# A decoder layer on one core: maxima issued ahead of operands and rows, the context's transposed text loaded instead of transposed on chip, two copies moved to ScalarE, and the last output split over two banks

## The chip, the core and the metric

The kernel runs on one core of a Trainium2 chip. The core has five engines with a program each: TensorE (PE in the profile, its weight loads PEld), VectorE (DVE), ScalarE (ACT), GpSimd (POOL) and SyncE (SP), which here does nothing but issue transfers on its queue. They meet at semaphores. The metric is the device time of one execution in microseconds (us), as the median of several runs.

## The reference

B = 8 sequences of T = 256 rows with D = 256 columns go through three stages, each followed by a layer norm. All is float32.

```python
x = layernorm(x + attn(x))             # causal attention, 16 heads of 16, with biases
x = layernorm(x + xattn(x, ctx_1024))  # slot attention on a context, 3 iterations
x = layernorm(x + ffn(x))              # 16 experts of 64, the best 4 for each row

# attn: att = softmax(mask(q k^T / 4)); y = att v; y @ w_proj + b_proj
# xattn: Pn = rmsnorm(ctx); k = Pn Wk^T; v = Pn Wv^T
#   3 times: softmax(rmsnorm(slots) Wq^T k^T / 16) over the slots, divided by its
#   sum over the context + 1e-6; updates = attn v; slots = gru(updates, slots)
# ffn: gates = 4 best of sigmoid(x sel^T), normalised; sum of gate * relu(x key_e) value_e
```

## The kernel before

**Precision.** Each float32 operand of a product is kept as two float32r tiles, HI and LO, and a product is three matmuls (`split3`). HI is written by ACT, LO = value - HI by DVE or POOL. A chain of "copy to HI, subtract to LO" stands behind every transposed text.

**Stage 1, attention**, is one long unrolled list of `quad`s: QUADS = 32, four to a sequence, each of three `third`s, with `period, place = divmod(quad, 8)`, so that a period is two sequences. The scores are computed twice. `natural(quad + 4)` makes them with rows on partitions, four quads ahead, and DVE takes the row maxima from them. Once two quads are done, PE transposes the maxima (job "neg", L1906), ACT copies them to `negT` (`maxima_out`, it raises `neg_ok`), and SP moves them as row K_ROWS = 96 of `q_op` (`maxima(hh)`, L519, two transfers of 4 KB for each half sequence hh = quad // 2). `turned(quad)` (L1872, L1876) then makes the scores transposed with the maxima already subtracted by that row. It waits for the maxima's landing at quad = 2 * hh.

`q_op` and `k_op` of sequences 1 to 7 take a way through memory. `write_q(pair, b)` and `write_k(pair, b)` (L489, L490, L497, L498) write three transfers of 256 KB each into `q_rows` and `k_rows`. `operands(n, half)` (L506, L509) waits for both to have landed (`rows_out`) and for the last reader of the buffer (`t_mm`), and then reads 768 KB back. All of this, the input rows (`load_x`, L475) and the maxima are issued by SP in one written order; a wait in it holds up all that stands behind. What SP issues at each quad is set by `place`: at place 0 `operands(2p+1, 1)`, `write_q(p+1, 0)`, `load_x`; at place 1 `write_k(p+1, 0)`; at place 2 `operands(2p+2, 0)`, `write_q(p+1, 1)`; at place 4 `operands(2p+2, 1)`, `load_x`; at place 6 `operands(2p+3, 0)`. After each of the even places stands `maxima(quad // 2 + 1)`.

**Stage 2, slot attention.** For a pair of sequences, `cross(i)` runs UNITS = 6 units u, alternating between the pair's two sequences (j = u % 2). PE computes scores for unit u + 1 (L1991), scales (L2000), the products with the attention weights (`inputs(u)`, L2171), and the state's products (L448). In units 4 and 5 of a pair it also prepares the next pair's context: `context_text(i, j)` transposes the context with four PE transposes (L456) into a PSUM bank, ACT and DVE make `cT_hl` from that bank, and keys and values follow. `c_in` holds the context as loaded; ACT takes squares of it for the norm (`c_sq`). The first pair's context is prepared in the last quads of stage 1 (`first_context`). Banks are handed on by lists (`jobs2`, `FIRST_BANK`): a job waits until the last job's reader in the same bank is done. `scales` (key "rb") and the second `context_text` share bank 1.

**Stage 3, experts.** `experts(i)` runs products with keys, gates and values for a pair. PE transposes x2 by way of a copy `x2f`, written by DVE in `text(i, j)`; for pair 1 this happens in the first `experts` call. The output of a sequence is two products of 24 matmuls, "half" (rows 0 to 127) and "o" (rows 128 to 255), in the two halves of one bank. When both are done, DVE adds x2, takes the moments, POOL makes the inverse deviation, DVE normalises into `y_out` and SP stores.

Of the kernel before, what the change touches and what calls it, by code (L numbers as in the profile page):

```python
# [17 lines left out]
ALU = mybir.AluOpType  # L18
# [4 lines left out]
P = 128  # L23
# [46 lines left out]
def decoder_layer(nc, x, xT, ctx, w_qkv, w_proj, wq, wk, wv, wihT, whhT, eselT, keys, values, cols, lines, out):  # L70
    stack = ExitStack()
    with stack:
# [64 lines left out]
        q_op = sb("q_op", [P, 2, 2, H // 2, T], F32R, where=sq_op)  # L137
# [18 lines left out]
        k_op = sb("k_op", [P, 2, H // 2, T], F32R, where=s1)  # L156
# [112 lines left out]
        rows_ok = sem("rows_ok")  # L269
# [15 lines left out]
        cT_mm, cT_hi, cT_lo = event("cT_mm", 2), event("cT_hi", 2), event("cT_lo", 2)  # L285
# [103 lines left out]
        for u in range(UNITS):  # L389
            jobs2 += (front(u + 1) if 0 < u < UNITS - 1 else front(u + 1)[1:]) + back(u)  # L390
            jobs2 += context(0)[:1] if u == 4 else []
            jobs2 += mid(u + 1) if u + 1 < UNITS else []
            jobs2 += front(UNITS)[:1] + context(0)[1:] + context(1)[:1] if u == 4 else []
        jobs2 += context(1)[1:2] + mid(UNITS)[:1] + context(1)[2:] + [(("uT", 0), 2, x2_ok, 2, 1)] + front(UNITS + 1)[:1]
# [29 lines left out]
        LAST_TEXT = (0, 2)  # L424
        jobs3 = []
# [43 lines left out]
        def _(sp):  # L469
# [43 lines left out]
            def maxima(hh):  # L513
# [3 lines left out]
                after(sp, rows_ok, 2 if hh == 0 else 0)  # L517
# [23 lines left out]
            for quad in QUADS_AND_TAIL:  # L541
# [32 lines left out]
                if quad % 2 == 0 and 0 <= quad // 2 + 1 < 2 * B:  # L574
# [1757 lines left out]
```

## Time and profile before

| what | value |
|---|---|
| median of 3 runs | 668.17 us (667.05 to 669.31) |
| the profiled execution's own time | 666.62 us |
| its span (the profile's times count from its start) | 664.9 us |
| PE busy | 621.7 us, 93% |
| DVE, ACT, POOL busy | 74%, 49%, 34% |
| stage 1 | up to about 233 us |
| stage 2 | about 233 to 545 us |
| stage 3 | from about 545 us |

The rows below come from the page of the profile and from views of its trace. A view of the chain that ended last gives start, duration and what was run or waited for. A timeline gives start, duration, engine, line, operation, output <- input, and in brackets the engine's idle time before it with what ended it. "SPq" is the time in which SP's queue takes in a transfer, not the transfer itself. PEclk is the TensorE clock that was granted, as a share of 2.4 GHz: 1.00 is that level, 0.50 is 1.2 GHz.

### The profile page before, as it was taken

What the parts mean: (1) busy time and instruction counts of PE and PEld (TensorE: products, weight loads), DVE (VectorE), ACT (ScalarE), POOL (GpSimd) and SP (SyncE); (2) the same over time, 40 slices, a digit from 0 to 9 for tenths busy, and PEclk for the clock granted to TensorE, in tenths of its full rate; (3) what the DMA queues carried; (4) which work ended last, traced back from release to release, by engine and by line L of the source; (5) the groups of instructions that cost most, each with busy time, mean ns of one, the idle gap of its engine ahead of it and who ended that gap; (6) DMA issues with size and microseconds to landing.
All of it is one profiled execution on the core that took longest, in us unless ns stands there. A gap on an engine that the chain in (4) does not pass through costs nothing.

```text
span 664.9 us, 13964 instructions
## 1 busy us (share of the span) xinstructions
PE 621.7 (93%) x5064; PEld 565.3 (85%) x5064; DVE 493.7 (74%) x1039; ACT 327.0 (49%) x734; POOL 225.2 (34%) x274
## 2 busy tenths in 40 slices
PE   5988998998999999999999999999999998899996
PEld 4766787776767989999899998999989988799996
DVE  4755474674764788879888799887999888767653
ACT  5444553553575355655556555565566644231320
POOL 9402332432453251422223232232312213352543
PEclk9799898997999999999999999999999999999999
DMA  8634646357400040010000000000000000042240
GB/s 283 203 103 146 173 135 190 93 173 217 121 18 1 1 160 0 2 33 2 0 0 0 32 0 0 0 0 0 0 1 1 1 1 1 16 147 82 80 157 34
DMA packets 31374, 43.34 MB, mean 65 GB/s; under 512 B 3072, under 2 KB 18912, under 8 KB 31328
## 3 DMA queue, kind: packets, MB, share of 16 engines
q1 hardware_dynamic: 31328, 42.73, 21.1%
q8 instruction: 28, 0.46, 0.3%
q14 instruction: 18, 0.15, 0.1%
HBM read 29.39 MB, written 13.21 MB: 64 GB/s over the span
## 4 chain that ended last, share of the span: by engine, by line
PE 56%; DVE 13%; issue 13%; DMA 5%; SPq 5%; POOL 4%; ACT 3%; DVEq 0%; POOLq 0%; ACTq 0%
PE bank L448 26%; PE bank L2171 11%; PE bank L1991 4%; POOL hid_hl L801 3%; DMA k_rows<-k_hl 3%; PE bank L1891 2%; DMA q_op<-negT 2%; PE bank L1977 1%; PE bank L456 1%; PE bank L1849 1%; PE bank L2008 1%; SPq L519 1%; PE bank L1856 1%; PE bank L1872 1%; PE bank L2000 1%
## 5 line engine op out<-in xcount | busy, mean ns | idle before, releaser
L448 PE MATMUL bank<-slots_hl,whhT_hl 128*128 128x256 f32 x864 | 113.1, 284 | 0.0
L448 PEld LDWEIGHTS bank<-slots_hl,whhT_hl 128*128 128x128 f32 x864 | 105.5, 188 | 2.4 <-ACT gate_z L1104 1.0
L1293 DVE TENSOR_REDUCE neg_max<-bank 128x2 f32<-128x512 f32 (+1 forms) x96 | 65.7, 690 | 55.2 <-PE bank L1858 41.3
L2171 PE MATMUL bank<-attn_hl,vg_hl 128*128 128x256 f32 x864 | 105.7, 280 | 0.1
L2171 PEld LDWEIGHTS bank<-attn_hl,vg_hl 128*128 128x128 f32 x864 | 100.9, 188 | 4.3 <-ACT attn_hl L815 3.9
L870 ACT ACTIVATE pT<-bank 128x512 f32<-128x512 f32 x96 | 56.9, 598 | 57.7 <-PE bank L1872 41.7
L682 POOL TENSOR_SCALAR_AFFINE_SELECT pT<-pT 128x512 f32<-128x512 f32 x64 | 40.6, 638 | 117.5 <-ACT pT L870 117.4
L696 POOL TENSOR_TENSOR sq<-sq 128x256 f32<-128x256 f32 x24 | 18.1, 754 | 170.6 <-ACT sq L1089 130.3
L801 POOL TENSOR_TENSOR hid_hl<-hid,hid_hl 128x512 fp32r<-128x512 f32 x32 | 40.9, 1303 | 25.8 <-ACT hid_hl L815 25.7
L448 PE MATMUL bank<-x2T_hl,keys_hl 128*128 128x256 f32 x384 | 48.6, 284 | 0.0
L448 PE MATMUL bank<-values_hl,hid_hl 128*128 128x256 f32 x384 | 47.8, 281 | 0.3 <-DVE x L1567 0.3
L448 PEld LDWEIGHTS bank<-x2T_hl,keys_hl 128*128 128x128 f32 x384 | 46.8, 191 | 0.1
L448 PEld LDWEIGHTS bank<-values_hl,hid_hl 128*128 128x128 f32 x384 | 45.6, 188 | 1.0 <-DVE x L1567 0.5
L1403 DVE RECIPROCAL inv_tot<-tot 128x256 f32<-128x256 f32 x24 | 42.1, 1753 | 0.8
L1872 PE MATMUL bank<-q_op,k_op 128*128 128x512 f32 x64 | 33.3, 526 | 6.7 <-DMA q_op<-negT 6.7
L1991 PE MATMUL bank<-slots_hl,kT_hl 128*128 128x256 f32 x288 | 39.4, 286 | 0.0
L448 PE MATMUL bank<-v_w_hl,cT_hl 128*128 128x256 f32 x288 | 37.2, 285 | 0.0
L448 PEld LDWEIGHTS bank<-v_w_hl,cT_hl 128*128 128x128 f32 x288 | 35.2, 188 | 0.8 <-issue 0.6
L1991 PEld LDWEIGHTS bank<-slots_hl,kT_hl 128*128 128x128 f32 x288 | 35.2, 189 | 0.0
L448 PE MATMUL bank<-xT_hl,wqkv_hl 128*128 128x512 f32 (+1 forms) x120 | 26.8, 371 | 7.8 <-DVE xT_hl L1231 6.9
L1094 ACT ACTIVATE gate_r<-bank,brz_col 128x256 f32<-128x256 f32 x48 | 20.2, 472 | 28.0 <-PE bank L2171 28.0
L815 ACT ACTIVATE hid_hl<-hid 128x512 fp32r<-128x512 f32 x32 | 19.5, 630 | 27.6 <-DVE hid L1765 22.2
(212 smaller groups left out, 1298.2 us busy)
## 6 DMA issues: line engine op xcount, KB each, us to landing
gate_rows<-gate_mem SPq DMA_DIRECT2D x48, 128.0 KB, 3.1
q_rows<-q_hl SPq DMA_DIRECT2D x21, 256.0 KB
k_rows<-k_hl SPq DMA_DIRECT2D x21, 256.0 KB
q_op<-q_rows SPq DMA_DIRECT2D x28, 192.0 KB, 3.2
k_op<-k_rows SPq DMA_DIRECT2D x14, 384.0 KB, 4.4
x_in<-in_x_dram SPq DMA_DIRECT2D x8, 256.0 KB, 6.6
c_in<-in_ctx_dram SPq DMA_DIRECT2D x8, 256.0 KB, 4.8
out_dram<-y_out SPq DMA_DIRECT2D x8, 256.0 KB, 2.8
```

What stands on the lines that cost most here:

```text
L448: mm = pe.matmul(dst, left(a), right(b), start=first and n == 0, stop=last and n == 2, skip_group_check=True)
L682: pool.affine_select(out=tile, in_=tile, compare_op=ALU.is_ge, fill=0.0, base=0, pattern=[[0, 4], [1, P]], channel_multiplier=-1).then_inc ...
L696: pool.tensor_tensor(sq[:, 0, :], sq[:, 0, :], sq[:, 1, :], ALU.add).then_inc(sq_sum, 1)
L801: pool.tensor_tensor(hid_hl[:, j, LO, 2 * g:2 * g + 2, :], hid[:, n % HIDDEN, :, :], f32(hid_hl[:, j, HI, 2 * g:2 * g + 2, :]), ALU.subtra ...
L815: return act.activation(dst, src, ACT.Copy, **kw)
L870: act.activation(dst, bank[2 + (3 * quad + third) % 2][:, :].rearrange("p (h n) -> p h n", h=4 if third == 2 else 2), ACT.Exp).then_inc(ex ...
L1094: r = act.activation(gate_r[:, c, :], halves(4)[:, c, :], ACT.Tanh, scale=0.5, bias=brz_col[:, c:c + 1])
L1293: dve.tensor_reduce(dst, src, AX.X, ALU.max, negate=True).then_inc(max_ok, 1)
L1403: dve.reciprocal(inv_tot[:, :], tot[:, :]).then_inc(it_ok, 1)
L1872: mm = pe.matmul(halves(b), k_op[:, n % 2, pair_of(quad, third), 0:P], q_op[:, n % 2, :, pair_of(quad, third), :], start=True, stop=True)
L1991: mm = pe.matmul(halves(b)[:, t, :], kT_hl[:, j, k_part, c, t * P:(t + 1) * P], slots_hl[:, j, s_part, c, :], start=n + t + c == 0, stop=n ...
L2171: mm = pe.matmul(halves(b)[:, m, :], vg_hl[:, j, v_part, 3 * t + r, q:q + P], attn_hl[:, j, at_part, t, :], start=n == 2 and a + m + t == ...
```

## The change

Four things change.

1. In SP's list, at places 0 and 4, `maxima` stands ahead of `operands`, `write_q` and `load_x`; at places 2 and 6 it stays behind them. `q_op` and `k_op` have 97 partitions in place of 128, so that two memsets of POOL and a wait of SP and PE for them (`rows_ok`) fall away.
2. `context_text` is gone from PE (8 blocks of four transposes). The host gives the transposed context too (`ctxT`), and SP loads it over the context in `c_in` once the squares are taken (`turned_context`, 8 more transfers of 256 KB). ACT and DVE make `cT_hl` from `c_in`, and the banks that the transposes used are no longer in the lists.
3. The two `x2f` copies for pair 1 move from DVE in the first `experts` to ACT in unit 4 of the last `cross`.
4. For the last sequence, the product "o" goes to bank 4 (`LAST_BANK`) in place of the second half of bank 3, and DVE adds x2 and takes the moments of each half by itself (`last_output`).

```diff
-        q_op = sb("q_op", [P, 2, 2, H // 2, T], F32R, where=sq_op)
+        q_op = sb("q_op", [K_ROWS + 1, 2, 2, H // 2, T], F32R, where=sq_op)
...
+            def turned_context(i, j):
+
+                sp.wait_ge(c_sq, due(2, i, j + 1))
+                sp.sem_inc(passed, 1)
+                sp.dma_start(c_in[:, j, :, :], rows(ctxT[i * 2 + j, :, :], NC)).then_inc(cT_arr[j], 16)
...
+                if quad in (QUADS - 6, QUADS - 5):
+                    turned_context(0, quad - (QUADS - 6))
+                if place in (0, 4) and 0 <= quad // 2 + 1 < 2 * B:
+                    maxima(quad // 2 + 1)
                 if place == 0:
                     if 1 <= 2 * period + 1 < B:
                         operands(2 * period + 1, 1)
...
-                if quad % 2 == 0 and 0 <= quad // 2 + 1 < 2 * B:
+                if place in (2, 6) and 0 <= quad // 2 + 1 < 2 * B:
                     maxima(quad // 2 + 1)
...
             def context_text_hi(r, j, first=False):
-                act.wait_ge(cT_mm, due(2, r, 2 + j + 1))
+                act.wait_ge(cT_arr[j], due(1, r, 2, step=16))
                 act.wait_ge(vg_mm, due(6, r, 6 + 3 * j))
-                copy(cT_hl[:, HI, :, :], halves(context_bank(("cT", j), first))).then_inc(cT_hi, 1)
+                copy(cT_hl[:, HI, :, :], c_in[:, j, :, :]).then_inc(cT_hi, 1)
...
                         expert_text_hi(0, 1, FIRST_TEXT[1])
+
+                        act.wait_ge(ss_mm, due(UNITS, i, UNITS))
+                        act.wait_ge(sc_ok, due(UNITS, i, UNITS))
+                        act.wait_ge(x2_ok, due(2, 1, 2))
+                        for j in range(2):
+                            copy(x2f[:, j, :, :], x2[:, (2 + j) * NT:(3 + j) * NT, :]).then_inc(xf_ok, 1)
...
+            def last_output(i):
+
+                def linked():
+                    dve.wait_ge(expert_chain, i * EXPERT_LINKS + next_link())
+                dve.wait_ge(y_ok, due(2, i, 1))
+                for t, (signal, count, b) in enumerate(((last_half, 1, 3), (o_mm, due(2, i, 2), LAST_BANK))):
+                    dve.wait_ge(signal, count)
+                    dve.tensor_tensor(u3[:, t, :], halves(b)[:, t, :], x2[:, i * (2 * NT) + NT + t, :], ALU.add).then_inc(expert_chain, 1)
+                    linked()
+                    dve.bn_stats(stats3[:, t, :], u3[:, t, :]).then_inc(expert_chain, 1)
+                    linked()
+                    dve.bn_aggr(mv3[:, t, :], stats3[:, t, :]).then_inc(expert_chain, 1)
+                    linked()
...
-                if first:
-                    text(1, 0)
-                    text(1, 1)
...
-                    if u == 4 and not last:
-                        context_text(i, 0)
...
-                        context_text(i, 1)
```

SP's list at quads 6, 8 and 9 (places 6, 0 and 1), before; `q_op<-negT` are the maxima:

```order
45 L519 DMA q_op<-negT 1x4x256 x2
46 L506 DMA q_op<-q_rows 48x2x512 x2
47 L509 DMA k_op<-k_rows 96x2x512
48 L489 DMA q_rows<-q_hl 8x16x512 x2
49 L490 DMA q_rows<-q_hl 8x16x512
50 L475 DMA x_in<-in_x_dram 128x2x256
51 L519 DMA q_op<-negT 1x4x256 x2
52 L497 DMA k_rows<-k_hl 8x16x512 x2
53 L498 DMA k_rows<-k_hl 8x16x512
```

The same place of SP's list after the change:

```order
44 L519 DMA q_op<-negT 1x4x256 x4
45 L507 DMA q_op<-q_rows 48x2x512 x2
46 L510 DMA k_op<-k_rows 96x2x512
47 L490 DMA q_rows<-q_hl 8x16x512 x2
48 L491 DMA q_rows<-q_hl 8x16x512
49 L476 DMA x_in<-in_x_dram 128x2x256
50 L498 DMA k_rows<-k_hl 8x16x512 x2
51 L499 DMA k_rows<-k_hl 8x16x512
```

The two transfers of `maxima(5)` have moved from behind seven transfers of 256 KB or so to in front of them (x4 is `maxima(4)` and `maxima(5)` side by side); their wait for `neg_ok` moves with them. The same happens at the other quads of place 0 and at those of place 4.

PE's list in units 4 and 5 of a `cross` in the loop, before:

```order
517 L1977 MATMUL bank<-mean_col,sq 128x1 x2
518 L448 MATMUL bank<-cT_hl,qk_w_hl 128x256 x12
519 L448 MATMUL bank<-v_w_hl,cT_hl 128x256 x36
520 L456 MATMUL bank<-ident,c_in 128x128 x4
521 L1991 MATMUL bank<-slots_hl,kT_hl 128x256 x12
522 L1943 REGISTER_ALU
523 L2000 MATMUL bank<-ident,s_rs 128x128 x2
524 L2171 MATMUL bank<-attn_hl,vg_hl 128x256 x36
```

And after:

```order
512 L2001 MATMUL bank<-mean_col,sq 128x1 x2
513 L1976 REGISTER_ALU
514 L449 MATMUL bank<-cT_hl,qk_w_hl 128x256 x12
515 L449 MATMUL bank<-v_w_hl,cT_hl 128x256 x36
516 L2015 MATMUL bank<-slots_hl,kT_hl 128x256 x12
517 L2024 MATMUL bank<-ident,s_rs 128x128 x2
518 L2192 MATMUL bank<-attn_hl,vg_hl 128x256 x36
```

The four transposes between the context's values and the scores are gone, as are the four behind `inputs(4)`; the order of the rest is as it was.

DVE's list at the end of the program, before (from the last sequence's addition to its norm):

```order
640 L1805 TENSOR_TENSOR u<-bank,x 128x512
641 L1549 BN_STATS stats<-u 128x6 x2
642 L1554 BN_AGGR mv<-stats 128x2 x2
643 L1557 TENSOR_SCALAR std<-mv 128x2
644 L1567 TENSOR_SCALAR y_out<-u,mv,std 128x256 x2
```

And after:

```order
638 L1769 TENSOR_TENSOR u<-bank,x 128x256
639 L1771 BN_STATS stats<-u 128x6
640 L1773 BN_AGGR mv<-stats 128x2
641 L1769 TENSOR_TENSOR u<-bank,x 128x256
642 L1771 BN_STATS stats<-u 128x6
643 L1773 BN_AGGR mv<-stats 128x2
644 L1775 TENSOR_SCALAR std<-mv 128x2
645 L1580 TENSOR_SCALAR y_out<-u,mv,std 128x256 x2
```

The first three rows now wait for "half" alone, so that only the second three and what follows stand behind the last product.

## Rows read from the trace of the kernel before

**Rows 1.** The page, busy time, share and instructions of each engine.
```profile
PE 621.7 (93%) x5064; PEld 565.3 (85%) x5064; DVE 493.7 (74%) x1039; ACT 327.0 (49%) x734; POOL 225.2 (34%) x274
```

**Rows 2.** The chain that ended last, 86 to 113 us: start, duration, what.
```profile
87.52 0.32 SPq L506
...
95.46 0.62 SPq L497
...
96.79 5.73 DMA k_rows<-k_hl
...
107.53 3.89 DMA q_op<-negT
```

**Rows 3.** Who waited for whom: us in total, times, longest.
```profile
PE bank L1872 <- DMA q_op<-negT: 6.7, 3, 2.5
```

**Rows 4.** Timeline of PE at the waits of stage 1.
```profile
111.46 0.50 PE L1872 MATMUL bank<-q_op,k_op 128*128 128x512 f32 x1 [2.46 <-DMA q_op<-negT]
...
184.31 0.66 PE L1849 MATMUL bank<-k_op,q_op 96*128 96x128 f32 x4
```

**Rows 5.** Timeline of ACT, the copies that raise `neg_ok` at place 0.
```profile
41.11 0.36 ACT L815 ACTIVATE negT<-bank 8x256 fp32r<-8x256 f32 x1
...
89.80 0.36 ACT L815 ACTIVATE negT<-bank 8x256 fp32r<-8x256 f32 x1
...
135.68 0.36 ACT L815 ACTIVATE negT<-bank 8x256 fp32r<-8x256 f32 x1
...
178.62 0.36 ACT L815 ACTIVATE negT<-bank 8x256 fp32r<-8x256 f32 x1
```

**Rows 6.** Issues of the maxima by SP: ns, least, median, most.
```profile
L519 SPq DMA_DIRECT2D q_op<-negT x32: 573/606/1752, 32.7 to 194.9; - x32
```

**Rows 7.** The chain that ended last, 48 to 60 us.
```profile
51.21 6.55 DMA k_rows<-k_hl
```

**Rows 8.** Timeline of SP, operands of periods 2 and 3.
```profile
133.40 0.79 SPq L506 DMA_DIRECT2D q_op<-q_rows  x2
...
177.17 0.43 SPq L509 DMA_DIRECT2D k_op<-k_rows  x1
```

**Rows 9.** The page, transfers: count, KB each, us from issue to landing.
```profile
k_op<-k_rows SPq DMA_DIRECT2D x14, 384.0 KB, 4.4
```

**Rows 10.** Stretches: length, PE busy (count), PEclk, DMA share, GB/s.
```profile
96.00:98.00 2.00, 2.00 (x28) 1.00 0.51 150
...
162.00:163.00 1.00, 1.00 (x6) 0.50 0.91 266
```

**Rows 11.** Timeline of DVE and PE in units 4 and 5 of the first `cross`.
```profile
295.11 1.53 DVE L1362 SCALAR_TENSOR_TENSOR vg_hl<-bank,c_rs,vg_hl 128x512 fp32r<-128x512 f32 x3
295.94 0.60 PE L456 MATMUL bank<-ident,c_in 128*128 128x128 f32 x4
...
296.30 1.62 PE L1991 MATMUL bank<-slots_hl,kT_hl 128*128 128x256 f32 x12
...
298.26 0.43 PE L2000 MATMUL bank<-ident,s_rs 128*128 128x128 f32 x2 [0.35 <-DVE cT_hl L1231]
```

**Rows 12.** Timeline at the first context, end of stage 1.
```profile
196.01 0.60 ACT L815 ACTIVATE cT_hl<-bank 128x512 fp32r<-128x512 f32 x1 [0.76 <-PE bank L456]
...
197.14 1.09 PE L1921 MATMUL bank<-ident,a_sb 128*128 128x128 f32 x8 [0.71 <-ACT a_sb L815]
```

**Rows 13.** Timeline around the `x2f` copies and their new place.
```profile
542.43 0.84 ACT L1094 ACTIVATE gate_r<-bank,brz_col 128x256 f32<-128x256 f32 x2 [0.49 <-PE bank L2171]
...
562.47 0.85 DVE L1747 COPY x2f<-x 128x512 f32<-128x512 f32 x2
...
568.69 3.10 PE L448 MATMUL bank<-values_hl,hid_hl 128*128 128x256 f32 x24 [0.32 <-DVE x L1567]
```

**Rows 14.** Timeline of DVE behind the last product.
```profile
658.58 0.69 DVE L1805 TENSOR_TENSOR u<-bank,x 128x512 f32<-128x512 f32 x1 [1.82 <-PE bank L448]
659.30 0.75 DVE L1549 BATCH_NORM_STATS2 stats<-u 128x6 f32<-128x256 f32 x2
```

More of the change, by code:

```diff
@@ L155, in decoder_layer @@
         x_in = sb("x_in", [P, 2, NT, D], where=s1)
-        k_op = sb("k_op", [P, 2, H // 2, T], F32R, where=s1)
+        k_op = sb("k_op", [K_ROWS + 1, 2, H // 2, T], F32R, where=s1)
         v_aug = sb("v_aug", [P, 3, NT, H, 2 * DH], where=s1)
@@ L268, in decoder_layer @@
         spot_in, spot_ok = sem("spot_in"), sem("spot_ok")
-        rows_ok = sem("rows_ok")
+        last_half = sem("last_half")
         set_mm, set_q, set_k = sem("set_mm"), sem("set_q"), sem("set_k")
@@ L284, in decoder_layer @@
         c_sq, c_mean, c_rstd, c_kept = event("c_sq", 2), event("c_mean", 2), event("c_rstd", 2), event("c_kept", 1)
-        cT_mm, cT_hi, cT_lo = event("cT_mm", 2), event("cT_hi", 2), event("cT_lo", 2)
+        cT_arr = [event(f"cT_arr{j}", 1, 16) for j in range(2)]
+        cT_hi, cT_lo = event("cT_hi", 2), event("cT_lo", 2)
         kT_mm, kT_hi, kT_lo = event("kT_mm", 2), event("kT_hi", 2), event("kT_lo", 2)
@@ L653, in _ @@
             for batch in range(2):
-                pool.memset(f32(k_op[K_ROWS:, batch, :, :]), 1.0).then_inc(consts, 1)
+                pool.memset(f32(k_op[K_ROWS:K_ROWS + 1, batch, :, :]), 1.0).then_inc(consts, 1)
             pool.wait_ge(consts, 16)
@@ L658, in _ @@
             pool.wait_ge(consts, 19)
-            for e in range(2):
-                pool.memset(f32(q_op[K_ROWS:, 0, e, :, :]), 0.0).then_inc(rows_ok, 1)
-            pool.wait_ge(rows_ok, 2)
             def rstd(i, var, ev, std, k, slot):
@@ L1148, in cross @@
                         expert_text_hi(0, 1, FIRST_TEXT[1])
+                        act.wait_ge(ss_mm, due(UNITS, i, UNITS))
+                        act.wait_ge(sc_ok, due(UNITS, i, UNITS))
+                        act.wait_ge(x2_ok, due(2, 1, 2))
+                        for j in range(2):
+                            copy(x2f[:, j, :, :], x2[:, (2 + j) * NT:(3 + j) * NT, :]).then_inc(xf_ok, 1)
                 if not last:
@@ L1346, in context_text_lo @@
                 dve.wait_ge(cT_hi, due(2, r, 2 + j + 1))
-                sub_hi(cT_hl[:, LO, :, :], halves(context_bank(("cT", j), first)), cT_hl[:, HI, :, :]).then_inc(cT_lo, 1)
+                sub_hi(cT_hl[:, LO, :, :], c_in[:, j, :, :], cT_hl[:, HI, :, :]).then_inc(cT_lo, 1)
             def context_keys_lo(r, j, first=False):
@@ L1747, in text @@
                 dve.tensor_copy(x2f[:, j, :, :], x2[:, bass.ds(i * (2 * NT) + j * NT, NT), :]).then_inc(xf_ok, 1)
+            def last_output(i):
[10 more added lines that the diff above has]
+                    linked()
+                dve.tensor_scalar(std3[:, 0, :], mv3[:, :, 1], LN_EPS, None, ALU.add).then_inc(var3, 1)
+                dve.wait_ge(stored[1], due(1, i, 1, back=1, step=16))
+                normal(i, lambda t: u3[:, t, :], mv3, std3, rstd3, 2, lambda t: y_out[:, 1, t, :], y_ok)
             def experts(i, last, first=False):
@@ L1802, in experts @@
                         route(i, i + 1, 1)
+                    if j and last:
+                        last_output(i)
+                        return
                     dve.wait_ge(o_mm, due(2, i, j + 1))
@@ L1868, in turned @@
                     pe.wait_ge(neg_in[hh % 2], 32 * (hh // 2 + 1))
-                    after(pe, rows_ok, 2 if hh == 0 else 0)
                 after(pe, exp_ok, fill - 1)
@@ L1944, in free_bank @@
                 return b
-            def context_text(r, j, first=False):
-                b = free_bank(r, ("cT", j), first)
-                pe.wait_ge(c_arr[j], due(1, r, 2, step=16))
-                transpose4(pe, b, lambda t, c: c_in[:, j, t, c * P:(c + 1) * P]).then_inc(cT_mm, 1)
             def context_keys(r, j, first=False):
@@ L2024, in first_context @@
             def first_context(quad):
[L2026 to L2028 removed]
+                if quad == QUADS - 3:
                     context_keys(-1, 0, True)
@@ L2275, in experts @@
                         pe.wait_ge(h_lo, due(8, i, 4 * j + 4))
+                        if last and j == 1 and t == 1:
+                            b = LAST_BANK
                         for m in range(NH):
@@ L2280, in experts @@
                             mm.then_inc(o_mm, 1)
+                        elif last and j == 1:
+                            mm.then_inc(last_half, 1)
             experts(0, False, True)
```

33 lines of the change are left out of this document (14 added, 19 removed).

## The prediction

> **What bounds the kernel now.** I read the page first. PE is busy 93% of the span [rows 1], so most of stages 2 and 3 is PE's own work, and what is left to win or lose there is a few tenths at each place where PE idles. Then I read who waits for whom. In stage 1 PE has one kind of wait on a transfer: L1872, `turned`, waits for the maxima three times, 6.7 us in total [rows 3]. The timeline shows the second of them, 2.46 us, ended at 111.46 [rows 4]; the three stand at quads 4, 12 and 20. The chain that ended last shows what such a wait hangs on. From 87.52 to 107.53 it runs through SP and the transfers and not through PE at all [rows 2]: SP issues operands of sequence 3, then rows of q, then x, then rows of k at 95.46; the rows of k land at 96.79 + 5.73 = 102.52; only then may SP issue the operands of sequence 4, behind them more rows of q and, last, `maxima(6)`, whose landing at 107.53 + 3.89 = 111.42 lets PE go on. So in stage 1 each period has one serial chain on SP's queue, and it starts with the `operands` of place 0.
>
> **The change part by part.**
>
> *Maxima ahead at place 0.* The maxima that the change brings forward (hh = 5, 9, 13 and 1) are not those that PE waits for: these (hh = 2, 6, 10) are issued at place 2, where the order stays. So the gain of having the others earlier is 0. The price is their wait. At quad 8 SP issued `operands` at 87.52 [rows 2], but `neg_ok` comes only with the copy at 89.80 + 0.36 = 90.16 [rows 5]. SP must now sit there, then issue two maxima of 0.606 us each [rows 6], and reaches `operands` at about 91.4: 3.9 us later. Period 2 is the same: 133.40 [rows 8] becomes 135.68 + 0.36 + 1.21 = 137.25 [rows 5, 6], 3.9 us later. Behind the `operands` stand `write_q`, `load_x` and `write_k`, and for them waits all that follows to `maxima(6)` and PE.
>
> How much of 3.9 us reaches PE? The lower bound is SP's own time. Before, the seven transfers took SP from 87.52 to 93.03 (the issue of the maxima) and `write_k` went at 95.46. After, the same 5.5 us from 91.4 end at 96.9, 1.4 us after 95.46. The upper bound is 3.9 us, if the queue's data and not the issue sets the landing. For this speaks that 768 KB of operands, 768 KB of q, 256 KB of x and 768 KB of k, 2.56 MB, went from 87.52 to 102.52, which is 171 GB/s, while in 96 to 98, where only writes of rows are left, the queue does 150 GB/s with a DMA share of 0.51 [rows 10]. It was working all the way. I take 3.9 for each of the two periods: **+7.8** (bounds 2.8 and 7.8).
>
> Which of the two bounds holds is where the Trainium skill has a say. Its page "DMA: Bandwidth & Descriptors", section "Two DMAs through the same engine are not ordered", says that in one queue of a DMA engine descriptors start in order; the section "Why a DMA increments its semaphore by 16 and not by 1" says that a transfer whose slowest dimension is 8 uses 8 of the 16 engines. The share of 0.51 agrees with the second. By both, rows of k can't pass rows of q on the same eight engines, and the cost is the upper bound; by the issue times alone it would be the lower one.
>
> *Period 0.* `maxima(1)` went at 41.11 + 0.36 = 41.47 at the earliest [rows 5], and now `operands(1, 1)` and `write_q(1, 0)` stand behind it, from 42.7. By the rate above, the 2.3 MB of operands, q and k take 13.5 us, up to 56.2. The rows of k landed at 51.21 + 6.55 = 57.76 anyway [rows 7], since k itself was late. So 0, and 0.5 as upper bound.
>
> *Quad 24.* `operands(7, 1)` moves by 178.62 + 0.36 + 1.21 = 180.2 against a start 0.83 ahead of 177.17 [rows 5, 8], 3.9 us. Its `k_op` then is issued at 181.1 and lands 4.4 us later [rows 9], at 185.5, while PE's `natural(30)` wanted it at 184.31 [rows 4]. **+1.2** (0.6 to 2.2). At place 4 the operands also move by 2 to 4 us, but they have two quads, over 8 us, until their reader: 0. The memsets and `rows_ok` are 0: the first maxima were issued at 32.7 [rows 6], far behind POOL's start-up. 97 partitions in place of 128 change no count of columns: 0.
>
> *Transposes off PE, in the loop (3 pairs).* Behind the transposes the scores start 296.30 - 295.94 = 0.36 us later [rows 11]. Behind the scores the scales waited 0.35 us for DVE's `cT_hl` because the two shared bank 1 [rows 11]; this wait is gone. The 0.36 us of unit 4's block comes too, but not at this place: the scores need bank 3, whose reader, the first of three DVE instructions from 295.11, ends after 0.75 at 295.9, and that time doesn't come from PE. So the scores start at 295.9 in place of 296.30 and `inputs(5)` 0.4 + 0.35 = 0.75 us earlier, three times: **-2.2** (-1.2 to -3.2, the latter if unit 4's block counts in full). The loads that replace them are issued behind `c_sq`, some 8 us ahead of their use, against landings of about 5 us: hidden. If they were not, each would stand before `cT_hl` for its lateness.
>
> *First context.* ACT waited 0.76 us for PE's transposes, and PE then 0.71 us for the `a_sb` that ACT makes behind them [rows 12]. **-0.6** (0 to -0.7). The second block, at 212.9, is hidden behind ACT's queue: 0. The 512 KB more at quads 26 and 27 run beside an empty queue.
>
> *x2f to ACT.* DVE loses 0.85 us at 562.47 [rows 13]. PE waits for a DVE norm at 568.69, so nearly all of it counts. ACT gains 1.2 us of copies just ahead of `gate_r` at 542.43, where it had 0.49 us to spare: 0.7 us late. DVE behind it has short idles, and PE works on other products meanwhile: 0 to 0.3. **-0.6** (-0.8 to +0.3).
>
> *Last output.* Behind the last product one addition of 128x256 in place of 128x512 and one of two statistics are left: half of 0.69 and half of 0.75 [rows 14]. **-0.7** (-0.3 to -0.8).
>
> **The sum.** 7.8 + 1.2 - 2.2 - 0.6 - 0.6 - 0.7 = +4.9 us against the profiled execution's own 666.62, so 671.5. The median of the runs stands 1.55 above that execution; with the same +4.9 it gives **673.1 us**. I forecast slower by 0.7%.
>
> **The rivals.**
>
> *Rows land by their own issue (ends faster).* The mechanism is in `write_k` of periods 1 and 2. Its landing came 102.52 - 95.46 = 7.06 us after its first issue, with all of q and x just ahead, and 51.21 + 6.55 with an empty queue was no quicker. If that is its own latency, and if SP's slow issues there (5.5 us for seven) were due to a full queue and shrink to 0.6 us each, `write_k` is issued at 91.4 + 4.2 = 95.6, as before. The 7.8 then is 0, quad 24 keeps its 1.2, and the time is 668.17 + 1.2 - 4.1 = 665.3. It decides from the point where 1.8 MB pass in under 5.6 us, which is 320 GB/s against the 150 seen with rows.
>
> *Half of it.* The issue bound: 2.8 + 1.2 - 4.1 = -0.1, 668.1, no change that one can measure.
>
> *The clock.* PE's longer waits of over 6 us (2.46 + 3.9) in place of 2.5. After the third wait of before the granted clock stood at 0.50, the 1.2 GHz level, still at 162 to 163, five us behind the end of the wait [rows 10]. Five us at half rate give 2.5 us more work time. If the second wait, and the new one at quad 26, get such a stretch in full, add about 2.5 to 3: 676. The page "TensorE: Matmul & The Clock Gate" of the Trainium skill, section "HAM oscillation", says that PE's idle gaps cost the clock anew each time; by it this rival is the likelier the longer the waits. Against it: the clock falls already in the shorter waits of before, so most of the price is in the old time.
>
> **How the numbers follow.** 0.60 for the sum as worked out (673.1, itself 670.5 to 675.5), 0.15 for the clock on top (676), 0.15 for rows by their own issue (665.3), 0.10 for half of it (668.1). The range must hold 0.8: it reaches from 666.5, which leaves out most of the faster case, to 677.5. A measurement of this kernel can't tell changes under some 0.3%, 2.0 us. Faster by more: 0.15. Within: 0.12, the half case and the low edge of the sum. Slower: 0.73.
>
> **What would show it.** In the changed trace: SP's issue of `operands` at quads 8 and 16 right behind the maxima and 3.9 us later against `t_mm`; rows of k landing over 9 us after their issue; PE's waits at L1872 of some 6 us for hh = 6 and 10 and an unchanged one for hh = 2; a new wait of about 1 us at `natural(30)`; in the loop no idle before the scales; the last norm some 0.7 us nearer to the last product. The forecast is wrong if the rows land 7 us after their issue as before, or if SP reaches `write_k` without delay; it is too low if PE's clock stays at its lower level for longer behind the waits.

## The result and the profile after

| what | before | changed |
|---|---|---|
| median | 667.44 us (6 runs, 665.71 to 669.31) | 672.30 us (6 runs, 671.36 to 675.35) |
| ratio | 1 | 1.0081, 95% interval 1.0053 to 1.0109 |
| span of the profiled execution | 664.9 us | 669.8 us |

The changed kernel is slower by 0.8%, 4.9 us both in the medians and in the spans. The forecast was 0.7%, +4.9 us. The agreement to a tenth of a us is luck, since the interval alone is nearly 2 us to either side. In this trace quad 24, period 0 and stage 3 each came out 1.8 to 2.7 us away from their terms, and these errors cancelled; the experiments below are mostly about those. An execution at a lower clock throughout (one of the kernel before, and the profiled one of run 10) does not enter the ratios.

The page of the changed kernel, busy time of each engine, against [rows 1]:

```profile
PE 620.0 (93%) x5016; PEld 563.3 (84%) x5032; DVE 493.9 (74%) x1038; ACT 328.0 (49%) x736; POOL 223.2 (33%) x272
```

PE's busy time falls by 1.7 us and its idle time grows by 6.6 us (43.2 to 49.8), so the loss is waiting. The busy time falls by less than the transposes took (32 matmuls, eight blocks like the 0.60 us of [rows 11]), because PE also ran longer at the lower level of the clock: the mean granted clock is 0.977 against 0.982, which is some 7 us more at 0.50, an estimate from these two means and spans. Who waited for whom in the changed kernel (us in total, times, longest), against the one row of [rows 3]:

```profile
PE bank L1901 <- DMA q_op<-negT: 7.2, 3, 3.2
PE bank L1879 <- DMA k_op<-k_rows: 7.2, 3, 3.0
```

L1901 is the old L1872, `turned`, and waits hardly longer than before (7.2 us for 6.7). New is L1879, `natural`, which waits for `k_op` three times. The timeline of PE has all six (start, duration, in brackets the wait):

```profile
66.19 0.49 PE L1901 MATMUL bank<-q_op,k_op 97*128 97x512 f32 x1 [0.97 <-DMA q_op<-negT]
...
108.63 0.66 PE L1879 MATMUL bank<-k_op,q_op 96*128 96x128 f32 x4 [3.00 <-DMA k_op<-k_rows]
...
112.56 0.80 PE L1901 MATMUL bank<-q_op,k_op 97*128 97x512 f32 x1 [3.03 <-DMA q_op<-negT]
...
158.27 1.11 PE L1879 MATMUL bank<-k_op,q_op 96*128 96x128 f32 x4 [2.54 <-DMA k_op<-k_rows]
...
162.57 0.80 PE L1901 MATMUL bank<-q_op,k_op 97*128 97x512 f32 x1 [3.19 <-DMA q_op<-negT]
...
191.17 0.66 PE L1879 MATMUL bank<-k_op,q_op 96*128 96x128 f32 x4 [1.63 <-DMA k_op<-k_rows]
```

The chain that ended last shows why, in the stretch that answers to [rows 2]:

```profile
87.20 0.36 ACT negT L822
...
87.58 0.57 SPq L519
...
88.20 0.57 SPq L519
...
88.89 0.37 SPq L507
...
94.69 1.13 SPq L498
...
96.49 6.97 DMA k_rows<-k_hl
...
108.64 3.88 DMA q_op<-negT
```

SP now waits for ACT's copy, issues the two maxima, and starts the operands at 88.89. At this place the changed kernel is 2.57 us ahead of the one before (quad 10's `turned` at 102.32 in place of 104.89), so 88.89 is 91.46 in the old count: 3.9 us later than 87.52, as forecast. The rows of k land at 96.49 + 6.97 = 103.46, that is 106.03 against 102.52, 3.5 us later.

How far the changed kernel is behind, from the starts of the same instruction in both timelines of PE, gives the whole account (clock 0.50 is the 1.2 GHz level):

| place | before | changed | behind | what happened there |
|---|---|---|---|---|
| `turned` of quad 4, its wait over | 67.31 | 66.19 | -1.12 | wait 0.97 for 1.78 |
| next `turned` | 71.10 | 68.45 | -2.65 | no stretch at clock 0.50 |
| `turned` of quad 12 | 111.46 | 112.56 | +1.10 | 3.00 + 3.03 for 2.46 |
| next `turned` | 115.03 | 116.66 | +1.63 | longer at clock 0.50 |
| `turned` of quad 20 | 157.38 | 162.57 | +5.19 | 2.54 + 3.19 for 2.50 |
| `turned` before `natural(30)` | 181.64 | 186.80 | +5.16 | |
| first `turned` of quad 28 | 192.90 | 201.39 | +8.49 | wait 1.63, then clock 0.50 |
| first `tot` product of stage 2 | 228.01 | 235.86 | +7.85 | first context, -0.64 |
| the same, last pair | 487.12 | 492.09 | +4.97 | loop, -2.88 |
| products with `eselT` | 567.28 | 571.06 | +3.78 | `x2f`, -1.2 |
| last values | 647.50 | 653.05 | +5.55 | clock 0.50 once, gates |
| end | 664.9 | 669.8 | +4.9 | last output, -0.65 |

### The profile page after: what moved, and what is told of

The parts are those of the page before. It is cut to its first block, busy times and chain, and to the rows that moved or that the text cites. A ratio compares the mean times of both kernels' runs of the same rounds, so it can differ in the third digit from the quotient of the medians.

```text
span 669.8 us, 13895 instructions
## 1 busy us (share of the span) xinstructions
PE 620.0 (93%) x5016; PEld 563.3 (84%) x5032; DVE 493.9 (74%) x1038; ACT 328.0 (49%) x736; POOL 223.2 (33%) x272
## 4 chain that ended last, share of the span: by engine, by line
PE 50%; DVE 15%; issue 14%; DMA 6%; SPq 5%; ACT 5%; POOL 4%; DVEq 0%; another core or an unknown queue 0%; ACTq 0%; POOLq 0%
PE bank L449 22%; PE bank L2192 9%; PE bank L2015 4%; DMA k_rows<-k_hl 3%; POOL hid_hl L808 3%; DMA q_op<-negT 2%; PE bank L1920 2%; PE bank L1901 1%; PE bank L2001 1%; PE bank L2032 1%; PE bank L1879 1%; PE bank L457 1%; DVE gate_r L1656 1%; SPq L519 1%; PE bank L1886 1%
## 5 line engine op out<-in xcount | busy, mean ns | idle before, releaser
L1901 PE MATMUL bank<-q_op,k_op 97*128 97x512 f32 x64 | 34.1, 539 | 7.2 <-DMA q_op<-negT 7.2
```

Of the source, the lines that this page charges most:

```text
L1901: mm = pe.matmul(halves(b), k_op[:, n % 2, pair_of(quad, third), 0:P], q_op[:, n % 2, :, pair_of(quad, third), :], start=True, stop=True)
```

## Experiments

Every ratio is to the kernel before, from runs on the same chip, with its 95% interval. All but the fourth keep the three other edits of the change and alter only SP's list; the edit of each is given against the changed kernel, that of the fourth against the kernel before. Single executions of the kernel before lie between 661.8 and 671.9 us, so a trace is one draw; its intervals and waits are worth more than its span. In each expectation, "theory" is what the author held likelier and "rival" the other reading.

### 1. The old order of the maxima, the other edits kept

```diff
-                if place in (0, 4) and 0 <= quad // 2 + 1 < 2 * B:
+                if quad % 2 == 0 and (quad in ()) and 0 <= quad // 2 + 1 < 2 * B:
...
-                if place in (2, 6) and 0 <= quad // 2 + 1 < 2 * B:
+                if quad % 2 == 0 and not (quad in ()) and 0 <= quad // 2 + 1 < 2 * B:
```

> The changed kernel with SP's maxima behind operands and rows at every place, as before; the other three edits stay. My theory: all of the loss is in this order. The changed trace stands 7.85 us behind at the first scale of stage 2; without it this goes and the first context's 0.6 stays, the loop gives 2.9 back, the tail 0.6, stage 3 loses about 0.5 at a DVE gate: 667.4 - 3.6 = 663.8, faster. Rival, the loss comes from the 768 KB or so of added context traffic and the edits on ACT: 668 or more. In the trace: SP's operands at quad 8 within 0.1 us of PE's release again, waits of PE for maxima three times 1.8 to 2.5, none for k_op.

Measured: 661.70 us, ratio 0.9932 (0.9901 to 0.9962). The theory's 663.8 (0.995) is inside the interval, the rival's 668 is not. The order costs 1.0081 / 0.9932 = 1.5%, 10 us, and the other edits together give 4.6 us; they were not run one by one. In the trace PE waits only at `turned` again, three times, 2.01, 3.10 and 3.12 us, the last two longer than the 2.5 us expected.

### 2. Maxima ahead at quad 0 alone

The edit is that of the first run with `(quad == 0)` in place of `(quad in ())`.

> As the first run, but the maxima of quad 0 alone stay ahead. The changed trace came 2.65 us earlier at the second half sequence of pair 1 (quad 4's wait 0.97 in place of 1.78, and no stretch of PE at the lower clock behind it). If the early maxima of quad 0, and the later operands and rows of q behind them, make that gain, this run is 2.3 to 2.7 us under the first: about 661.3, the fastest so far. Rival, that the shorter wait is scatter of one execution: equal to the first run within 0.5 us, 663.8.

Measured: 660.77 us, 0.9922 (0.9894 to 0.9950). 0.9 us under the first run, less than the intervals can tell. The traces settle more. The wait at quad 4 was 1.26 here and 0.97 in the changed kernel, but 2.00 in run 4, which has the maxima of quad 0 ahead too. With the old order at quad 0 it was 1.78 before, 2.01 in run 1, 1.68 in run 3, 2.25 in run 5, 0.56 in run 7, 1.35 in run 9 and 1.36 in run 11: the scatter of this wait is as large as the effect. What it costs depends on a step. The products behind it in the kernel before and in run 3 (timelines of PE, `wqkv` products behind the wait):

```profile
67.87 2.91 PE L448 MATMUL bank<-wqkv_hl,xT_hl 128*128 128x256 f32 x12
```

```profile
67.14 1.68 PE L449 MATMUL bank<-wqkv_hl,xT_hl 128*128 128x256 f32 x12
```

The same twelve matmuls took 2.91 us behind the wait of 1.78 and 1.68 behind the wait of 1.68. In the traces with waits of 1.78, 2.01 and 2.25 there they ran at the lower level of the clock, in the one with 2.00 (run 4) in part, 2.41 us, and in all those with up to 1.68 at the upper. So the -2.65 of the account is 0.3 of start, 0.8 of wait and 1.5 of clock, and it is luck of one execution as much as a gain of the change.

### 3. Maxima ahead at quads 8 and 16 alone

The edit is that of the first run with `(quad in (8, 16))`.

> As the first run, but maxima ahead at quads 8 and 16 alone. Theory, the queue's data sets when rows of k land: each period loses 3.6 us between quad 4 and quad 12's end, 7.2 in all, so 671.0. Rival, SP's own issue sets it: 1.4 each, 2.8 in all, 666.6. In the trace: PE waits at natural for k_op and at turned for maxima at quads 12 and 20, together some 5.5 us in each period.

Measured: 668.11 us, 1.0031 (1.0004 to 1.0058): 6.4 us over the first run, 3.2 for each period. The theory's 7.2 lies 0.8 off, the rival's 2.8 lies 3.6 off, outside the interval. PE's waits in this run:

```profile
109.81 0.83 PE L1879 MATMUL bank<-k_op,q_op 96*128 96x128 f32 x4 [3.13 <-DMA k_op<-k_rows]
...
113.73 0.79 PE L1901 MATMUL bank<-q_op,k_op 97*128 97x512 f32 x1 [2.64 <-DMA q_op<-negT]
...
159.76 0.66 PE L1879 MATMUL bank<-k_op,q_op 96*128 96x128 f32 x4 [3.43 <-DMA k_op<-k_rows]
...
163.80 0.80 PE L1901 MATMUL bank<-q_op,k_op 97*128 97x512 f32 x1 [3.14 <-DMA q_op<-negT]
```

### 4. The kernel before, with the new order alone

```diff
+                if place in (0, 4) and 0 <= quad // 2 + 1 < 2 * B:
+                    maxima(quad // 2 + 1)
                 if place == 0:
...
-                if quad % 2 == 0 and 0 <= quad // 2 + 1 < 2 * B:
+                if place in (2, 6) and 0 <= quad // 2 + 1 < 2 * B:
```

> The kernel before with the new order of maxima alone. Theory: stage 1 loses what it lost in the changed kernel, 7.85 plus the 0.5 that the first context gave back, and nothing returns later: 667.4 + 8.3 = 675.7. Rival, half of the loss needs the new context traffic at quads 26 and 27: 673 or less.

Measured: 679.95 us, 1.0195 (1.0148 to 1.0242), 9.9 to 16 us of loss. The rival falls: the loss needs none of the other edits. But the median is 4 us over the forecast, outside the interval, so the theory's size is not met either. Its trace waits for `k_op` at the same three quads:

```profile
112.96 0.66 PE L1851 MATMUL bank<-k_op,q_op 96*128 96x128 f32 x4 [2.32 <-DMA k_op<-k_rows]
...
163.12 1.11 PE L1851 MATMUL bank<-k_op,q_op 96*128 96x128 f32 x4 [2.92 <-DMA k_op<-k_rows]
...
196.00 0.66 PE L1851 MATMUL bank<-k_op,q_op 96*128 96x128 f32 x4 [1.78 <-DMA k_op<-k_rows]
```

All of its 13.2 us stand at the first `tot` product of stage 2 (241.22 for 228.01), and nothing is added later. Of these, 2.2 stand already at the first `turned` of quad 0 (42.15 for 39.91). This start lies between 39.33 and 42.15 in the traces, without regard to the order (42.13 in run 9, whose list is the old one up to there), so this part is scatter of one execution. Why 11 remain, where the changed kernel lost 7.85 + 0.64, is not shown.

### 5. The wait without the issues

On top of the edit of the first run:

```diff
+                if quad in (8, 16):
+                    sp.wait_ge(neg_ok, quad // 2 + 2)
                 if place == 0:
```

> As the run with the old order, but at quads 8 and 16 SP waits for neg_ok ahead of operands and issues nothing there; the maxima stay behind. It tells the price of the wait from that of the two issues. Theory, the queue's data sets the landing and every us of late start counts: start 2.64 later instead of 3.85, and the run with maxima ahead at the same quads lost 6.4 by 7.7 of late start, so 2 x (2.64 - 0.65) = 4.0: 0.9932 + 0.0060 = 0.999 of before, 665.7. Rival, SP's issue time sets it, and the wait is taken up by issues that were slow on a full queue: 0.5 or less, 662.2.

Measured: 667.21 us, 1.0011 (0.9985 to 1.0038), 5.3 us over the first run by the ratios. The theory's 0.999 is inside the interval, the rival's 662.2 (0.994) is not. Compared with the 6.4 of run 3 the wait by itself is most of the price, but the two do not lose it at the same places: here `maxima(5)` and `maxima(9)` went out late behind seven transfers, and PE waited for them at quads 10 and 18 (the first and the third row), while its wait at quad 12 (the second) shrank to 1.21:

```profile
101.03 0.50 PE L1903 MATMUL bank<-q_op,k_op 97*128 97x512 f32 x1 [1.29 <-DMA q_op<-negT]
...
114.12 0.49 PE L1903 MATMUL bank<-q_op,k_op 97*128 97x512 f32 x1 [1.21 <-DMA q_op<-negT]
...
147.99 0.49 PE L1903 MATMUL bank<-q_op,k_op 97*128 97x512 f32 x1 [2.21 <-DMA q_op<-negT]
```

So putting the maxima first does buy something once SP waits anyway. In the old order their readers had time to spare.

### 6. Maxima ahead where PE waits for them, place 2

The edit is that of the first run with `(quad == 0 or place == 2)`.

> Maxima ahead of operands at quad 0 and at place 2 (quads 2, 10, 18, 26, those for which PE waits at quads 4, 12 and 20), behind them elsewhere. SP idles at place 2 until rows of k land (96.8 to 102.5), while neg_ok comes at 100.1, so the maxima cost the operands nothing and land before PE's turned. Theory: PE's three waits of 2.0, 3.1 and 3.1 go, and part of the half clock behind them: 660.8 - 8 = 652 to 654, ratio 0.98. Rival, natural takes the wait over: k_op lands just when PE wants it (issue 104.3, wanted 108.8), so its landing is later by the 1.2 of issues: gain 4 or less, 657 and up.

Measured: 662.58 us, 0.9940 (0.9913 to 0.9968). The theory falls; even the rival's 4 us did not come. The three waits for maxima at quads 4, 12 and 20 are gone, and these stand in their place:

```profile
75.44 0.66 PE L1879 MATMUL bank<-k_op,q_op 96*128 96x128 f32 x4 [0.48 <-DMA k_op<-k_rows]
...
107.23 0.66 PE L1879 MATMUL bank<-k_op,q_op 96*128 96x128 f32 x4 [0.73 <-DMA k_op<-k_rows]
...
119.99 1.12 PE L1879 MATMUL bank<-k_op,q_op 96*128 96x128 f32 x4 [3.68 <-DMA k_op<-k_rows]
...
167.82 1.11 PE L1879 MATMUL bank<-k_op,q_op 96*128 96x128 f32 x4 [4.09 <-DMA k_op<-k_rows]
```

SP's timeline of this run shows what the wait at 119.99 hangs on (start, duration, issue):

```profile
98.41 1.29 SPq L519 DMA_DIRECT2D q_op<-negT  x2
101.92 0.79 SPq L507 DMA_DIRECT2D q_op<-q_rows  x2
...
108.83 1.16 SPq L499 DMA_DIRECT2D k_rows<-k_hl  x1
110.30 1.91 SPq L507 DMA_DIRECT2D q_op<-q_rows  x2
112.26 0.43 SPq L510 DMA_DIRECT2D k_op<-k_rows  x1
```

The maxima cost nothing, as said: they went out at 98.41 while SP had to wait until 101.92 for rows. But behind them stand the second sequence's rows of q and k (`write_q` of place 2 and `write_k` of place 3, which the list of places above leaves out), issued up to 109.99. The operands of place 4 follow them at once, from 110.30, and their `k_op`, issued at 112.26, landed 7.7 us later, at 119.96; at place 0 and place 2 this took 4.1 and 4.4. In run 1 the `k_op` of place 4 was as slow, 7.2 us (114.73 to 121.9), but there PE had been held up at quad 12 and wanted it only at 122.59. Here it was at `natural(18)`, in quad 14, from 116.31 on. The wait at `turned` was hiding this one.

### 7 and 8. load_x behind write_k

On top of the edit of the first run (run 7) and of the sixth (run 8):

```diff
                     if 1 <= period + 1 < PAIRS:
                         write_q(period + 1, 0)
-                    if 2 <= 2 * period < B:
-                        load_x(2 * period)
-                elif place == 1 and 1 <= period + 1 < PAIRS:
-                    write_k(period + 1, 0)
+                elif place == 1:
+                    if 1 <= period + 1 < PAIRS:
+                        write_k(period + 1, 0)
+                    if 2 <= 2 * period < B:
+                        load_x(2 * period)
```

> As the run with the old order, but load_x of place 0 is issued behind write_k of place 1, so 256 KB are out of the way of rows of k. Theory, the queue's data: 256 KB at 176 GB/s are 1.5 us, rows of k land that much earlier, PE's waits at quads 12 and 20 are 1.6 in place of 3.1: 661.7 - 2.9 = 658.8. Rival, rows land 7 us after their own issue: write_k waits for nothing but SP and is issued 0 to 1.4 us earlier; if it is not (k_lo sets it), nothing: 661.7.

> Both: maxima ahead at quad 0 and place 2, load_x behind write_k. Theory: once PE waits for no maxima, k_op just in time is next, and 1.5 us more slack there give 0 to 1 us: 652 to 653. Rival, the chain from operands of place 0 to k_op at quad 10 bounds the period: 2 to 3 under the run without the move of x.

Measured: 660.78 us, 0.9922 (0.9895 to 0.9949) with the old order, and 662.52 us, 0.9943 (0.9912 to 0.9975) with maxima ahead at place 2. Neither differs from its partner beyond the intervals, and both theories are refuted (658.8 and 652 to 653), as is the rival of run 8 (2 to 3 us under run 6). In run 7 `write_k` was issued 7.13 us after the operands and not 7.52, and its rows landed 7.35 us after that: 14.48 in all for 15.26 at quad 8, half of the 1.5 us that the theory gave, and 14.85 for 14.96 at quad 16, nothing.

### 9. Maxima ahead at quad 24 alone

The edit is that of the first run with `(quad == 24)`.

> As the run with the old order, with maxima ahead at quad 24 alone. My prediction gave this place 1.2 us. The changed kernel's trace shows 1.63 of wait for k_op at 191.17 and a stretch at 0.50 of the clock behind it, 3.3 in all, of which 0.6 to 0.8 came back in the first context. Theory: 2.5 to 3 over the old order (0.9932), ratio 0.997. Rival, the prediction's 1.2 alone: 0.995.

Measured: 663.75 us, 0.9939 (0.9916 to 0.9962), 0.5 us over the first run by the ratios, 1.3 by the medians. The 0.995 of the prediction's 1.2 is inside the interval, the theory's 0.997 is outside. The wait is there, and as long as in the changed kernel:

```profile
187.32 0.66 PE L1879 MATMUL bank<-k_op,q_op 96*128 96x128 f32 x4 [1.88 <-DMA k_op<-k_rows]
187.86 0.58 PE L1901 MATMUL bank<-q_op,k_op 97*128 97x512 f32 x1
```

What differs is the clock. Stretches of PE behind this wait, in run 9 and in the changed kernel (length, PE busy, PEld, DVE, ACT, POOL, then the granted clock):

```profile
187.00:189.00 2.00, 1.68 (x11) 1.45 (x13) 0.69 (x1) 0.52 (x2) 0.00 (x0) 1.00 0.45 134
189.00:191.00 2.00, 2.00 (x27) 1.40 (x25) 1.59 (x3) 2.00 (x6) 0.64 (x1) 1.00 0.01 2
```

```profile
192.00:194.00 2.00, 2.00 (x9) 1.49 (x8) 1.21 (x2) 0.94 (x3) 0.00 (x0) 0.53 0.16 56
194.00:196.00 2.00, 2.00 (x17) 1.66 (x19) 0.75 (x2) 1.31 (x3) 0.63 (x1) 0.62 0.01 4
```

Behind a wait of 1.88 the clock stayed at 1.00 (2.4 GHz), behind one of 1.63 it stood at 0.53, the mean of two us that were nearly all at the 1.2 GHz level. The length of the last wait alone does not decide it.

### 10. Maxima ahead at place 4 alone

The edit is that of the first run with `(place == 4)`.

> Maxima ahead at place 4 alone (quads 4, 12, 20, 28). My prediction costs this at 0, since the operands there have two quads until their reader. Theory: no new wait of PE at natural, 0.993 of before. Rival, the run with maxima ahead at place 2 showed k_op late by 3.7 at quad 14, so there is little slack behind place 4 either and some 1 us at each of quads 12 and 20 comes: 0.996.

Measured: 662.37 us, 0.9901 (0.9865 to 0.9938), by the medians alone 0.993. The rival's 0.996 is outside the interval: no loss, and the prediction's 0 holds. There is no trace to use, so PE's waits here are not shown.

### 11. One more transfer of 256 KB ahead of write_k

On top of the edit of the first run (the memory `spare_rows`, its semaphore and a wait for it at the very end are left out here):

```diff
                         write_q(period + 1, 0)
+                    if quad in (8, 16):
+                        sp.dma_start(rows_of(spare_rows, 0)[:, :, 0, :], f32(q_hl[:, HI, 0, :, :]).rearrange("p c t -> p (c t)")).then_inc(spare, 16)
```

> As the run with the old order, plus one more transfer of 256 KB in the form of the rows (8x16x512, the HI of q into memory that nobody reads) behind write_q at quads 8 and 16. It prices the queue's data by itself. Theory, the queue's data: 256 KB at the 180 GB/s of rows alone are 1.45 us, the time from SP's operands to the landing of rows of k goes from 15.3 to 16.7, PE's waits grow as much: 2.5 to 3 in all, ratio 0.997. Rival, SP's issue and the own latency of write_k: 0.6 of issue each, 1.2, ratio 0.995, and the time from write_k to its landing stays 7.7.

Measured: 664.45 us, 0.9960 (0.9934 to 0.9987), 1.9 us over the first run by the ratios. This lies between the two and tells them apart poorly. The intervals on SP's timeline do better. They run from the issue of the operands at quads 8 and 16 to the first issue of `write_k`, over SP's three issues of it, and from the end of the last one to the next operands (which wait for the landing):

| kernel | to `write_k` | its three issues | to the landing | sum |
|---|---|---|---|---|
| before | 7.94, 7.23 | 1.98, 1.97 | 5.09, 5.09 | 15.01, 14.29 |
| run 1, old order | 7.52, 7.84 | 1.96, 1.89 | 5.78, 5.23 | 15.26, 14.96 |
| run 2, quad 0 | 7.49, 7.32 | 1.89, 1.89 | 5.98, 5.35 | 15.36, 14.56 |
| run 9, quad 24 | 7.82, 7.59 | 1.98, 1.90 | 5.21, 5.35 | 15.01, 14.84 |
| run 5, wait alone | 7.21, 7.50 | 2.14, 1.89 | 4.82, 5.78 | 14.17, 15.17 |
| run 6, place 2 | 7.71, 7.30 | 2.11, 1.89 | 6.32, 5.90 | 16.14, 15.09 |
| run 7, x behind | 7.13, 7.12 | 1.92, 1.94 | 5.43, 5.79 | 14.48, 14.85 |
| run 8, place 2 and x | 7.12, 7.12 | 2.01, 2.31 | 5.59, 6.04 | 14.72, 15.47 |
| run 12, quad 0 and x | 7.12, 7.13 | 2.25, 1.97 | 5.51, 5.78 | 14.88, 14.88 |
| run 11, 256 KB more | 8.67, 8.55 | 1.90, 1.89 | 4.99, 4.99 | 15.56, 15.43 |
| changed | 5.80, 5.43 | 3.63, 3.01 | 5.16, 5.70 | 14.59, 14.14 |
| run 3 | 5.58, 5.65 | 3.77, 3.72 | 5.34, 5.33 | 14.69, 14.70 |
| run 4 | 5.21, 5.62 | 3.20, 3.67 | 5.45, 5.09 | 13.86, 14.38 |

From the end of the last issue to the landing it is the same in both orders, 4.8 to 6.3 us. What differs is in front of it. With the maxima ahead at quads 8 and 16 (the last three rows) `write_k` begins 5.2 to 5.8 us after the operands in place of 7.1 or more, but its three issues then take SP 3.0 to 3.8 us in place of about 2. SP's timeline at quad 9, in run 1 and in the changed kernel:

```profile
95.72 1.28 SPq L498 DMA_DIRECT2D k_rows<-k_hl  x2
97.06 0.62 SPq L499 DMA_DIRECT2D k_rows<-k_hl  x1
```

```profile
94.69 1.75 SPq L498 DMA_DIRECT2D k_rows<-k_hl  x2
96.49 1.83 SPq L499 DMA_DIRECT2D k_rows<-k_hl  x1
```

So nearly all of the earlier start is given back while SP issues, the sum shrinks by only some 0.5 us, and the late start comes through almost in full. That SP is slow there because the queue is still full is the likely reading; no run separates it.

Nor was the queue as full as the theory had it. The added 256 KB lengthen the sum by 0.40 and 0.77 us over the means of before and of runs 1, 2 and 9, and not by 1.45. And while only rows of k are left, the DMA share is the same in the changed kernel as in [rows 10], but more is moved:

```profile
100.00:102.00 2.00, 2.00 (x26) 1.52 (x19) 1.66 (x4) 1.35 (x3) 0.84 (x2) 1.00 0.53 205
```

It is 205 GB/s here at a share of 0.53, and 150 there at 0.51 (177 at 0.53 in the two us that follow). The share tells that these DMA engines were busy, not how much more they could have moved.

### 12. Quad 0 ahead and load_x behind write_k

The edit is that of the seventh run with `(quad == 0)` in place of `(quad in ())`.

> The two moves that looked useful, maxima ahead at quad 0 only and load_x behind write_k, with the three other edits. Each alone gave 0.9922 against 0.9932 for the old order, within its interval. Theory: 1 us each, 0.991, 660. Rival: neither is real, 0.993.

Measured: 661.44 us, 0.9904 (0.9878 to 0.9929). The theory's 0.991 and the rival's 0.993 differ by less than the interval, so nothing is decided.

## Why the prediction was right, step by step

By the ratios of the runs both halves of the sum came out near their terms: the order of the maxima cost 10 us where 7.8 + 1.2 = 9.0 were given, and the other edits gave 4.6 us where 4.1 were. The parts of each half did less well.

- **Maxima ahead at place 0, 7.8.** Measured in the account: from -2.57 to +1.63 and from +1.66 to +5.16, 7.7 us, about 0.5 of it clock; 6.4 in run 3. The start came 3.9 us late as forecast, and 3.5 of it reached the landing. The upper bound was the right one to take. The lower one had the start of `write_k` nearly right (5.80 and 5.43 us after the operands for 5.5) and failed on what came behind it: SP's issues of it took 3.63 and 3.01 us in place of 2. The reason given for the upper bound, that the queue "was working all the way", does not carry it: 150 GB/s was not what the queue could do (205 in the changed kernel), and run 11 found room in it. The rule of the Trainium skill (page "DMA: Bandwidth & Descriptors", section "Two DMAs through the same engine are not ordered") that descriptors of one queue of an engine start in order agrees with the landing that did not come earlier with an earlier `write_k` (9.11 us behind its first issue in run 3, 7.74 in run 1), but does not single it out. The sign "over 9 us" was missed narrowly: 8.79 and 8.71.
- **Where PE would feel it.** The prediction looked for waits of 6 us at `turned`. They came in two parts, 3.00 at `natural` for `k_op` and 3.03 at `turned`. It had not asked when the operands behind the rows are wanted: in run 1 `k_op` is issued at 104.29 and wanted at 108.84, 4.5 later, which is its landing time [rows 9]. The sum was not touched by that.
- **Quad 24, +1.2.** The wait was 1.63 in the changed kernel and 1.88 in run 9. SP's issue came at 186.37 - 5.16 = 181.2, as forecast, and the landing took 4.8. In the account the place cost 3.3, since the clock fell behind the wait; in run 9 it did not, and 0.5 (by the medians 1.3) came out. The clock belonged into its upper bound of 2.2.
- **Period 0, 0.** The changed kernel was 2.65 us ahead there in this trace. Run 2 gives 0.9, not clear of zero, so this gain is mostly luck of the one execution. The step missed that the wait at quad 4 stands at the edge at which the clock falls or stays, 1.5 us either way.
- **Loop, -2.2.** Measured -2.88 here and -2.8 in run 1 (from 228.24 to 484.56). The mechanism was right and its size a little low, 0.96 us for each pair in place of 0.75: in the rows that answer to [rows 11] the scales wait no more, and the scores wait 0.30 for DVE's `vg_hl`.

```profile
303.58 1.65 PE L2015 MATMUL bank<-slots_hl,kT_hl 128*128 128x256 f32 x12 [0.30 <-DVE vg_hl L1375]
...
305.07 0.38 PE L2024 MATMUL bank<-ident,s_rs 128*128 128x128 f32 x2
```

- **First context, -0.6.** Measured -0.64.
- **x2f, -0.6.** A mis-sized term: it gave 1.2 us, twice as much. PE waited before at two places of this chain that the prediction did not count, for `x2f` itself and for `x2T_hl`:

```profile
563.13 0.63 PE L456 MATMUL bank<-ident,x2f 128*128 128x128 f32 x4 [0.68 <-DVE x2f L1747]
...
567.28 0.86 PE L448 MATMUL bank<-x2T_hl,eselT_hl 128*16 128x256 f32 x6 [2.61 <-DVE x2T_hl L1231]
```

  The first wait is gone and the second is now 2.26. What stage 3 then lost was not in the prediction. Behind the wait for `x2T_hl` PE's clock fell:

```profile
571.06 1.44 PE L449 MATMUL bank<-x2T_hl,eselT_hl 128*16 128x256 f32 x6 [2.26 <-DVE x2T_hl L1244]
572.29 0.63 PE L2289 MATMUL bank<-gateT_hl,spread 128*128 128x256 f32 x2
572.73 3.75 PE L449 MATMUL bank<-values_hl,hid_hl 128*128 128x256 f32 x24
```

  The six products took 1.44 in place of 0.86, and 24 values 3.75 in place of 3.10 [rows 13]. Such a stretch stands there in 8 of 11 traces with the edit and in neither of the two without it. Whether the edit brings it was not settled: runs 1, 3 and 5 have the edit and not the stretch. Two waits for gates, 0.94 and 0.76, where the kernel before has one of 0.81 and run 1 has 0.18 twice, took about 0.9 more. In all stage 3 lost 1.8 us behind this place, to which the sum gave nothing.
- **Last output, -0.7.** From the end of the last product to the end 6.36 before and 5.71 now, -0.65.
- **The rivals.** Rows landing some 7 us after their first issue is refuted by the changed kernel's 8.79 and 8.71, and by the medians of runs 1 and 3, with which "half of it" falls too. The clock came, at quad 26 (1.6 us) and in stage 3, and was repaid by the clock that did not fall at quad 4.

The parts do not add up: quads 8 and 16 cost 6.4, quad 24 0.5 to 1.3, quad 0 gave 0.9 and place 4 cost nothing, yet together they cost 10. Each ratio is uncertain by some 2 us, and where the clock falls changes from one execution to the next; whether these make the missing 3 to 4 us, or the places act on each other, stays open.

Not tried: whether rows written by all 16 DMA engines would loosen the whole chain. The DMA share of 0.51 to 0.53 while they go out is that of about half of them, the rows' transfer has 8 as its outer size, and turning it needs another order of q's and k's partitions.

## What to carry to other kernels

Before a small transfer is put first in a queue, ask what it waits for: if its wait ends later than that of the work behind it, the queue pays the difference. It was 3.9 us here, and nearly all of it reached the engine that was bound, first at the reader that had no slack and not at the one that had waited before. A wait that is removed pays only as far as the next one in the same chain: run 6 took away the three waits that make up 8.2 us in run 1, and gained nothing. And a rate read off a busy stretch (150 GB/s at a DMA share of 0.51) is not the most that the queue can do (205 at 0.53): it takes a run with more in the queue, like run 11, to tell.

## What was not expected of the hardware

Whether the clock falls behind a short idle time of PE can't be read off that time alone. At quad 4 it goes by the length of the wait in all thirteen traces that can be used: two without a wait and seven with 0.56 to 1.68 us stayed at 1.00, four with 1.78 to 2.25 fell to 0.50. At quad 26 a wait of 1.88 us left it at 1.00 in one kernel, and 1.63 brought it down in another. Twelve matmuls then take 2.91 us in place of 1.68. With the products around them that is some 1.5 us for each such stretch, as much as most edits of this study are worth. The start of stage 1 alone moves by 2.8 us from trace to trace. A difference of a few us between the spans of two single traces therefore says little.
